# Six fused transformer layers on one core: normalising on another engine, a new order of the first loads, and new stage priorities

## The reference

```
L0:    y = attention(x, ctx, ctx, mask) @ Wo.T + bo + x;  x = (y - mean) * rsqrt(var + 1e-12) * ln_g + ln_b
L1:    y = attention(x, ctx, ctx) @ Wo.T + bo + x;        x = (y - mean) / sqrt(var + 1e-5) * gamma + beta
SELF:  h = LN1(x);  x = x + causal_attention(h, h, h) @ m_proj_w + m_proj_b
CROSS: x = x + attention(LN2(x), ctx, ctx) @ c_proj_w + c_proj_b
FFN:   x = x + relu(LN3(x) @ f_w1 + f_b1) @ f_w2 + f_b2
L3:    x = x + attention(LN4(x), ctx, ctx) @ ternary(Wo).T + bo     (Wq, Wk, Wv ternary too)
```

## Time and profile before

| | us |
|---|---|
| median of three runs | 1471.36 (1467.45 to 1472.52) |
| the profiled execution | 1471.28 |
| span of its profile | 1469.5 |

### The profile page before, as it was taken

How to read it: one execution, slowest core, us unless ns; L and a number is a source line. 1 busy time by engine, 2 the same in 40 slices (tenths; PEclk the granted TensorE clock), 3 DMA queues, 4 the chain that set the end, 5 groups by cost and what they waited for, 6 DMA issues and landing times.

```text
span 1469.5 us, 44720 instructions
## 1 busy us (share of the span) xinstructions
PE 1372.2 (93%) x19500; PEld 1158.0 (79%) x19500; DVE 1093.1 (74%) x2032; ACT 809.8 (55%) x1327; POOL 564.4 (38%) x579
## 2 busy tenths in 40 slices
PE   4899889899989999999999999998999999999998
PEld 4777777777877778787888877787899999788786
DVE  2776777798888876767777798788576666878674
ACT  3667555656656556465555666665433333566654
POOL 5854333544354345233333343122277555212100
PEclk9999999999999999999999999999999999999999
DMA  7211000100000010000000010000000000001000
GB/s 253 69 51 54 26 12 15 36 24 9 9 15 9 2 31 17 2 2 2 2 2 17 9 44 9 8 15 23 1 16 1 1 1 2 23 23 37 24 23 30
DMA packets 17034, 34.94 MB, mean 24 GB/s; under 512 B 2503, under 2 KB 7879, under 8 KB 16327
## 3 DMA queue, kind: packets, MB, share of 16 engines
q1 hardware_dynamic: 16839, 32.09, 7.0%
HBM read 27.89 MB, written 4.19 MB: 22 GB/s over the span
## 4 chain that ended last, share of the span: by engine, by line
PE 66%; DVE 22%; ACT 5%; issue 4%; POOL 1%; DMA 1%; SPq 1%; DVEq 0%; ACTq 0%; POOLq 0%
DVE s_nm L1064 10%; PE ps L690 9%; PE ps L755 8%; PE ps L783 5%; PE ps L769 5%; PE ps L717 5%; PE ps L582 5%; PE ps L635 4%; PE ps L734 4%; PE ps L594 4%; PE ps L607 3%; PE ps L695 2%; DVE s_KH L1021 2%; ACT s_PU L904 2%; PE ps L714 2%
## 5 line engine op out<-in xcount | busy, mean ns | idle before, releaser
L1064 DVE TENSOR_REDUCE s_nm<-ps 128x8 fp32r<-128x960 f32 (+1 forms) x352 | 397.7, 1168 | 75.0 <-PE ps L635 41.9
L904 ACT ACTIVATE s_PU<-ps 120x1024 f32<-120x1024 f32 (+1 forms) x288 | 279.5, 1026 | 144.4 <-PE ps L695 144.3
L1195 POOL TENSOR_TENSOR s_xs<-s_xs,s_rowv 128x512 f32<-128x512 f32 x96 | 125.0, 1302 | 285.6 <-DVE s_nt L984 266.7
L690 PE MATMUL ps<-s_Qs,s_KH 32*120 32x256 f32 (+2 forms) x4608 | 194.8, 293 | 29.4 <-DVE s_nm L1064 16.5
L690 PEld LDWEIGHTS ps<-s_Qs,s_KH 32*120 32x120 f32 (+1 forms) x4608 | 157.4, 183 | 58.0 <-DVE s_nm L1064 20.1
L913 ACT ACTIVATE s_Os<-ps 128x512 f32<-128x512 f32 x160 | 95.1, 597 | 115.6 <-PE ps L717 71.2
L755 PE MATMUL ps<-s_W,s_oT 128*128 128x256 f32 x960 | 137.6, 294 | 6.3 <-DVE s_oT L997 5.2
L582 PE MATMUL ps<-s_xT,s_W 128*128 128x256 f32 x960 | 135.5, 291 | 4.4 <-POOL s_xT L1201 3.0
L717 PE MATMUL ps<-s_PU,s_Vp 120*32 120x256 f32 x2048 | 131.2, 384 | 8.8 <-DVE s_nm L1064 5.8
L755 PEld LDWEIGHTS ps<-s_W,s_oT 128*128 128x128 f32 x960 | 122.5, 194 | 19.3 <-DVE s_oT L997 13.7
L582 PEld LDWEIGHTS ps<-s_xT,s_W 128*128 128x128 f32 x960 | 120.7, 191 | 11.5 <-issue 4.5
(11 more groups left out here) (98 smaller groups left out, 2540.8 us busy)
## 6 DMA issues: line engine op xcount, KB each, us to landing
s_cf<-ctx_t SPq DMA_DIRECT2D x32, 240.0 KB, 2.6
s_ws<-weights SPq DMA_DIRECT2D x28, 256.0 KB, 2.8
s_xs<-x_nat SPq DMA_DIRECT2D x4, 1024.0 KB, 10.8
s_nt<-x_t SPq DMA_DIRECT2D x16, 256.0 KB, 2.7
out<-s_xs SPq DMA_DIRECT2D x16, 256.0 KB, 2.0
s_rowv<-rows SPq DMA_DIRECT2D x6, 512.0 KB, 4.0
s_mi<-mask SPq DMA_DIRECT2D x8, 120.0 KB, 3.4
s_ident<-ident SPq DMA_DIRECT2D x1, 64.0 KB, 1.9
```

The costliest lines, as they stand in the source:

```text
L690: e.matmul(banks[j][0:n, wide * x:wide * x + wide], kz[row[j], lk, g, c, k0:k0 + n], q[row[j], lq, g, qs_], start=(x == 0 and y_ == 0), st ...
L904: t = e.activation(P_of(i, k)[0:n, :, :], pair("B", i, k)[0:n, :, :], ACT.Exp, scale=0.25)
L1064: e.tensor_reduce(o, v, AX.X, ALU.max, negate=True).then_inc(sem["max"])
L1195: e.tensor_tensor(xs[:, b, :, :], xs[:, b, :, :], row2(layer, 0), ALU.add).then_inc(sem["pool"])
```

## The change

- N and ln move from VectorE to ScalarE, as `activation(Identity)` with scale rs and bias -mean * rs: the same two instructions of 128 x 256 for each stage, 192 in all. GpSimd makes the bias in place of the mean, by two more instructions on 128 x 2 in each rs (96 of them): a product and a change of sign.
- The low part of L0's four weights is made by VectorE (stage Wd) instead of GpSimd (Wl).
- The constants are one array and one transfer of 128 x 306; the mask columns are a transfer of their own in SP's planned order, with its own semaphore.
- The wants of the first loads: K's weights first, then the context and the mask, Q's weights, the mask columns, x^T, V's weights, the row vectors, O's weights; the x blocks later than before.
- WANT has a value for each layer for most stages; STAY goes from 0.158 to 0.006; LONG gets values for the moved stages.

The diff, without the parts that follow from these (names of semaphores, dispatch tables, arguments):

```diff
 
 
-WANT = dict(Xl=-1.31, xT=-3, cT=-4, mi=-4, bo=-0.54, N=2.96, T=-0.96, Q=0.18, Qh=2.79, Ql=0.43, K=-0.21, Kh=1.11, Kl=0.59,
-            K0=-0.06, V=0.68, Ve=2.57, mf=-0.74, A=0.45, max=0.14, M=-0.05, mTe=0.55, B=0.86, exp=0.68, cap=1.77, PV=1.79,
-            PVe=2.42, ON=2.33, ONe=1.93, OT=2.98, O=-0.19, y=2.45, st=6.41, rs=0.41, ln=1.69, lng=4.37, F1=-0.76, Fa=0.46,
-            Fv=-2.33, Hl=0.58, F2=2.43, out=2.2, Th=-2.92, Tl=-1.16, OTh=-0.54, OTl=1.4, Ch=-3, Cl=-3)
-
-
-LONG = dict(xT=.6, cT=.6, mi=.6, ws=.6, row=.6, x=.6, out=.6, bo=1.3, N=.65, T=.44, Th=.48, Tl=.62, Xl=1.3, Q=1.43, Qh=.74, Ql=.8, K=1.35, K0=.87,
+WANT = dict(Xl=2.33, xT=-3, cT=-4, mi=-4, bo=(-1.38, -4.6, 0.82, 0.54, 4.02, -2.73), N=(0, 0, 7.36, 5.95, 4.46, 10.15),
+            T=(0, -1.03, -0.22, -0.68, -0.56, -0.75), Q=(0.31, -0.09, 0.08, 0.12, 0, 0.89), Qh=(4.65, 5.69, 4.82, 2.33, 0, 7.3),
+            Ql=(4.24, 5.24, -0.37, 1.41, 0, -4.79), K=(0.04, 0.95, -0.74, -0.32, 0, 0.14), Kh=(7.03, 3.26, 8.4, 3.42, 0, 7.23),
+            Kl=(13.58, 11.97, 2.38, 0.81, 0, 4.94), K0=(-2.55, -0.13, 1.77, -5.48, 0, -4.59), V=(1.53, 1.27, 1.39, 1.09, 0, 0.96),
+            Ve=(7.29, 6, 8.04, 5.94, 0, 5.43), mf=-9.45, A=(0.94, 0.26, -0.22, 0.9, 0, -4.03),
+            max=(1.44, -8.07, -2.39, -8.27, 0, -4.55), M=(-4.4, -9.75, -3.93, -3.85, 0, -3.9), mTe=(-3.16, 5.59, 2.13, -1.13, 0, 8.06),
+            B=(0.16, -1.34, -2.27, -1.09, 0, -3.55), exp=(1.98, 1.72, -0.9, 3.06, 0, 2.4), cap=2.08,
+            PV=(2.68, 2.11, 1.48, 2.16, 0, -0.32), PVe=(2.06, -0.55, 4.1, 4.9, 0, 4), ON=(1.61, 2.48, 3.07, 2.54, 0, -2.38),
+            ONe=(-0.48, -5, -3.72, -3.42, 0, -8.34), OT=(4.03, 1.43, 3.08, 1.76, 0, 3.6), O=(-3.16, -1.62, -1.42, 2.41, 0, 0.38),
+            y=(3.92, 3.63, 1.68, 3.03, 1.58, 1.11), st=(7.15, 8.77, 12.99, 7.5, 9.79, 0), rs=(1.67, -0.61, 1.09, -0.07, 5.79, 0),
+            ln=(11.5, 3.83, 0, 0, 0, 0), lng=(0.08, 5.07, 0, 0, 0, 0), F1=-0.96, Fa=8.14, Fv=8.74, Hl=2.08, F2=1.38, out=2.2,
+            Th=(-5.03, -8.61, -5.12, -8.43, -10, -10.16), Tl=(0, 1.26, -0.81, 1.24, -1.59, 2.94),
+            OTh=(-9.48, -6.82, -11.62, -5.25, 0, -8.56), OTl=(-2.41, 0.77, -6.29, -1.15, 0, -2.19),
+            Ch=(-1.04, -0.8, 0, -8.83, 0, -3.71), Cl=(0.77, -2.69, 0, 0.79, 0, -6.45))
+
+
+LONG = dict(mci=.5, xT=.6, cT=.6, mi=.6, ws=.6, row=.6, x=.6, out=.6, bo=1.3, N=.72, T=.44, Th=.48, Tl=.62, Xl=1.3, Q=1.43, Qh=.74, Ql=.8, K=1.35, K0=.87,
             Kh=1.17, Kl=1.25, V=1.43, Ve=.67, Ch=.5, Cl=1.25, mf=.3, A=.69, max=1.07, M=.22, mTe=.28, B=.95, exp=.91, cap=.67, PV=.87,
-            PVe=.48, ON=.44, ONe=.64, OT=.44, OTh=.48, OTl=.62, O=1.43, y=.6, st=1.05, rs=1.04, ln=.65, lng=2.6, F1=2.86, Fa=.72, Fv=.79,
-            Hl=2.43, F2=2.86, wb=.5, wa=.2, wg=.75, Wh=.52, Wl=1.3, qs=.57, qm=.05, qa=1.5, qw=4.1)
+            PVe=.48, ON=.44, ONe=.64, OT=.44, OTh=.48, OTl=.62, O=1.43, y=.6, st=1.05, rs=1.6, ln=.72, lng=2.6, F1=2.86, Fa=.72, Fv=.79,
+            Hl=2.43, F2=2.86, wb=.5, Wd=.6, wa=.2, wg=.75, Wh=.52, Wl=1.3, qs=.57, qm=.05, qa=1.5, qw=4.1)
 LAND = dict(xT=2.5, cT=2.5, mi=2.5, ws=3.0, row=3.5, x=7.0, out=3.0)
 
 ARRAY = dict(A="rows", B="rows", PV="columns")
 TURN = .19
-STAY = 0.158
+STAY = 0.006
 NEXT = .11
 
 
@@ -54,6 +64,17 @@
 def half_pairs(i, hf):
 
     return [2 * hf, 2 * hf + 1] + ([4, 5] if layer_of(i) == "SELF" else [])
+
+
+def want_of(name, i):
+
+    v = WANT[name]
+    return v[LAYERS.index(layer_of(i))] if isinstance(v, tuple) else v
+
+
+def rest_of(layer):
+
+    return "Wd" if layer == "L0" else "Wl"
...
-                add("DVE", "N", after=[x_ready(i), ("rs", i - B, 1 if layer_of(i - B) == "L1" else 0)],
+                add("ACT", "N", after=[x_ready(i), ("rs", i - B, 1 if layer_of(i - B) == "L1" else 0)],
...
-            add("PE", "Q", after=[x_t, ("Wl", layer, 0)],
+            add("PE", "Q", after=[x_t, (rest_of(layer), layer, 0)],
...
-            add("DVE", "ln", after=[("rs", i, 0)])
+            add("ACT", "ln", after=[("rs", i, 0)])
...
-    p.add("SP", "row", 0, want=-3.5, rings=[("row", 0, layer_end("L0", "lng"))])
-    p.add("SP", "x", 0, want=-3.4)
-    for k in range(1, 4):
-        p.add("SP", "x", k, want=-2 + k)
+    p.add("SP", "row", 0, want=-2.6, rings=[("row", 0, layer_end("L0", "lng"))])
+    p.add("SP", "mci", 0, want=-3.3)
+    for k in range(4):
+        p.add("SP", "x", k, want=-1 + 1.2 * k)
...
-        for m in range(4):
-            at = start + (.5 if n else .05) * m
-            p.add("SP", "ws", layer, m, want=at, rings=[("ws", (layer, m), [("Wl", layer, m)])])
+        for m in (1, 0, 2, 3) if n == 0 else range(4):
+            at = start + .5 * m if n else {1: -9, 0: -3.9, 2: -2.7, 3: -.5}[m]
+            p.add("SP", "ws", layer, m, want=at, rings=[("ws", (layer, m), [(rest_of(layer), layer, m)])])
...
+            if layer == "L0":
+                p.add("DVE", "Wd", layer, m, want=at, after=[("Wh", layer, m)])
+            else:
+                p.add("POOL", "Wl", layer, m, want=at, after=[("Wh", layer, m)])
...
+N_CST = 16
...
+        cst = sb("cst", [128, 306])
+        ident, caus, hsel, pick, colv, c2 = (cst[:, a:b] for a, b in ((0, 128), (128, 256), (256, 258), (258, 262), (262, 282), (282, 306)))
...
+            n_pool += {"bo": 1, "cap": 1, "rs": 4, "lng": 2, "Xl": 1, "Cl": 1, "Hl": 1, "Wl": 1, "qw": 3}[name]
...
+            if n == "L0":
+                return sem["Wd"], nth("Wd", n, m)
...
+            def N(i):
+                was = ring["nt"].before[i]
+                if layer_of(was) == "L0":
+                    w.wait_ge(sem["pool"], pool_ops["Xl", was, 0])
+                else:
+                    w.wait_ge(sem["T"], nth("T", was))
+                w.wait_ge(sem["pool"], pool_ops["rs", i - B, 1 if layer_of(i - B) == "L1" else 0])
+                w.wait_ge(*x_value(i))
+                b = i % B
+                for q in range(2):
+                    t = e.activation(nt[slot("nt", i)][:, q, :], xs[:, b, q, :], ACT.Identity, bias=mv[:, b, q, 0:1],
+                                     scale=rs[:, b, q:q + 1])
+                t.then_inc(sem["N"])
+
+            def ln(i):
+                b = i % B
+                w.wait_ge(sem["pool"], pool_ops["rs", i, 0])
+                for q in range(2):
+                    t = e.activation(xs[:, b, q, :], xs[:, b, q, :], ACT.Identity, bias=mv[:, b, q, 0:1], scale=rs[:, b, q:q + 1])
+                t.then_inc(sem["ln"])
...
+            w.wait_ge(sem["d_mci"], 16)
             e.tensor_scalar(mcol[0:C, :], mci[0:C, :], 0.0, GONE / 4, ALU.is_equal, ALU.mult).then_inc(sem["cst"])
-
-            def N(i):
-                was = ring["nt"].before[i]
-                if layer_of(was) == "L0":
-                    w.wait_ge(sem["pool"], pool_ops["Xl", was, 0])
-                else:
-                    w.wait_ge(sem["T"], nth("T", was))
-                w.wait_ge(sem["pool"], pool_ops["rs", i - B, 1 if layer_of(i - B) == "L1" else 0])
-                w.wait_ge(*x_value(i))
-                b = i % B
-                for q in range(2):
-                    t = e.tensor_scalar(nt[slot("nt", i)][:, q, :], xs[:, b, q, :], mv[:, b, q, 0:1], rs[:, b, q:q + 1],
-                                        ALU.subtract, ALU.mult)
-                t.then_inc(sem["N"])
 
...
+            def Wd(n, m):
+                w.wait_ge(sem["Wh"], nth("Wh", n, m))
+                e.tensor_tensor(wv(n, 1, m), ws_of(n, m)[:, :, :], wv(n, 0, m).bitcast(f32), ALU.subtract).then_inc(sem["Wd"])
...
-            def ln(i):
-                b = i % B
-                w.wait_ge(sem["pool"], pool_ops["rs", i, 0])
-                for q in range(2):
-                    t = e.tensor_scalar(xs[:, b, q, :], xs[:, b, q, :], mv[:, b, q, 0:1], rs[:, b, q:q + 1], ALU.subtract, ALU.mult)
-                t.then_inc(sem["ln"])
...
+                behind()
+                e.tensor_tensor(mv[:, b, :, 0], mv[:, b, :, 0], rs[:, b, :], ALU.mult).then_inc(sem["pool"])
+                behind()
+                e.tensor_scalar(mv[:, b, :, 0], mv[:, b, :, 0], -1.0, None, ALU.mult).then_inc(sem["pool"])
...
-            for tile, src in ((hsel[:, :], headsel_d), (ident[:, :], ident_d), (caus[:, :], causal_d), (pick[:, :], pick_d),
-                              (colv[:, :], cols[:, 0:20]), (c2[:, :], cols[:, 20:44]), (mci[0:C, :], mask_t)):
-                e.dma_start(tile, src).then_inc(sem["d_cst"], 16)
+            e.dma_start(cst[:, :], consts).then_inc(sem["d_cst"], 16)
...
+            def mcols(i):
+                e.dma_start(mci[0:C, :], mask_t).then_inc(sem["d_mci"], 16)
```

More of the change, by code:

```diff
@@ L115, in add @@
         key = (name, i, k)
-        self.stages[key] = Stage(engine, key, at + (WANT[name] if want is None else want), LONG[name] if long is None else long,
+        self.stages[key] = Stage(engine, key, at + (want_of(name, i) if want is None else want), LONG[name] if long is None else long,
                                  list(after), list(rings))
@@ L268, in make_plan @@
```

(21 more changed lines are left out.)

14 lines of the change are left out of this document (3 added, 11 removed).

## The result

The changed kernel takes **1402.71 us** (median of four runs, 1402.28 to 1404.88) against 1471.94: ratio 0.954, 95% interval 0.952 to 0.956. The forecast was 1441 with a range from 1410: right in sign, too small by more than half, and 7 us outside the range. Rival B (1406) had named the time, with a chance of 0.12.

What follows compares the result with a forecast made beforehand. TensorE's own work was taken as the floor, leaving its 97.3 us idle, array turns and lower clock. Terms -10 - 16 + 4 - 10 + 2 = -30 us from 1471 gave 1441, range 1410 to 1466.

Steps and rivals of the forecast that it cites:

- Rival B: Whole kernel: most TensorE waits go; VectorE's relief -35, wants -20, start -10 us, giving 1406 us; chance 0.12.
- Start, -10 us: Kernel start: earlier context and K weights bring first K near 7.5, first scores near 15 us; -10, ends 0 and -16.
- Move, -16 on VectorE and +4 on ScalarE: N and ln: lighter VectorE cuts TensorE's waits, -16 us; ScalarE's added work delays exps and evacuations, +4 us.
- 30% less queueing: VectorE's queue: waiting goes as busy over idle share, 2.8 before and 2.0 after, giving -16 us.
- the 52.3 us of waits: TensorE's waits naming VectorE as releaser, 23 rows summed; expected to fall to near 36 us.
- The +4: ScalarE's queue: waits scaled by load, 2 us, plus some 2 for ln pairs waiting on rs; ends 0 and +33.
- Wants, -10, ends -35 and +20: Compute queues' order: wants by layer save a quarter of the first two layers' idle time, -10 us.
- The +2 for STAY: TensorE's array shapes: lower STAY changes visits little, as most wants lie further apart than 0.158; +2 us.
- Rival A: Whole kernel: only the start pays, VectorE waits being of necessary order; 1461 us, chance 0.18.
- rival C: ScalarE's queue: N or ln pairs ahead of needed exps make it the one to wait for; +11, 1482 us; chance 0.10.

Runs made afterwards that it cites:

- fitted orders: Kernels with wants fitted to their division of work: N, ln on ScalarE, five including the changed kernel, mean 1406.4 us; on VectorE, three, mean 1416.0 us.
- the two searches: New start, old STAY, wants searched from the old ones, two random sequences per engine: N, ln on VectorE 1409.31 and 1422.21 us, on ScalarE 1410.42 and 1405.04.
- the worst misfit: Kernel before with only the new wants by layer and STAY 0.006; old start, N and ln on VectorE: 1520.52 us.
- The table: All eight combinations of start, move and wants (with STAY), each old or new, including the kernels before and after: 1402.7 to 1520.5 us.

## Why the prediction was wrong

**Start, -10 us.** Right in size and mechanism: -8.3 alone and -12.2 on top of move and wants, though only -2.7 beside the move with the old wants. First K at 7.99 (forecast 7.5), scores at 17.76 (15). The difference is the mask columns and the order Q, Q, V before the first scores. What I hadn't looked at is the weight that came late at 26.81.

**Move, -16 on VectorE and +4 on ScalarE.** Here the reasoning failed. The engine sums came near: VectorE 989.0 (forecast 984), ScalarE 897.7 (910), GpSimd 600.0 (622). For ScalarE that is partly luck: an instruction takes 0.60 us and not 0.52, 192 of them are 115 us, and the engine's busy time rose by only 88. The 128 of N alone cover 69.4 us of time instead of 128 x 0.597 = 76: neighbours overlap in the profile. But "30% less queueing" treats VectorE as a queue fed at random, while the engines work off lists that the planner makes anew when a stage changes its engine. With the old wants it made a plan 16 us longer, and the run with the move alone took 2.7 us more, not 12 less; of the 52.3 us of waits, 47.6 remained. The prediction had the relief without the new lists. The relief may be in there: that kernel is 59 us longer than its plan, the one before 73, and beside the new start it is 58 and 66. That would be 14 and 8 us, near the -12 forecast and the 8 to 10 among fitted orders. It is argued from the plan, whose durations of N are themselves wrong (0.65 us where VectorE takes 1.28 for a pair, 0.72 where ScalarE takes 1.08), and no run shows it. The +4 was also scaled by load alone; with the same busy over idle as for VectorE it would have been about +7.

**Wants, -10, ends -35 and +20.** This is the term that was mis-sized, and the main step that failed: beside the move, the new wants are worth -60 and -69 us. Orders from the two searches are worth 54 and 41 us with N on VectorE (1463.6 to 1409.3 and 1422.2) and 67 and 61 with N on ScalarE (1471.9 to 1405.0 and 1410.4), and the worst misfit costs 49. Both ends were too near. I had reasoned from how much idle time one set of wants for all layers leaves, and had taken the coarse reading of the wants, as priorities. I wrote that the new order can't be worked out from the trace; it could be from the kernel. Run without the chip, the planner gives 1398.9 us before and 1354.2 after, 45 us less, where the whole forecast was 30. I had also left out TensorE's busy time as something an order can shorten: it was to stay within 5 us of 1372, and fell by 28.6. The +2 for STAY has no run of its own; its reason, a visit more or less, isn't borne out: the array changes fell from 696 to 652.

**The sum.** The steps were added. The table shows that they can't be: the wants are worth -69 or +48 by what stands beside them. Rival A is out: idle time outside the first 32 us is 42.3 us and not 77. Rival B came within 4 us of the time, but by luck: its 65 us were to be idle time, 35 of them waits for VectorE that the move takes, and 28.6 of the 69.8 came out of the busy time instead; rival C's mechanism, waits for ScalarE, rose from 16.2 to 24.6 us and not to 40. The rule of the Trainium skill, "ScalarE: Activation LUTs", section Rules for kernel authors, that adds and multiplies belong on VectorE, agrees with the median instruction, 0.41 us there against 0.59 on ScalarE. It didn't decide the time: with fitted orders the kernels with N on ScalarE are 8 to 10 us shorter in the mean.

## What to carry to other kernels

Where a kernel's queues are laid out by a planner from fixed durations, an edit of the work and the order of the work can't be priced apart: refit the order for each side of a comparison, or the comparison measures the luck of the order (here 50 us either way, against about 10 for the edit). Run the planner before forecasting; its own length had the sign and most of the size of what a new set of priorities did. When a stage moves to another engine, look at the new lists before crediting the relief. To learn whether a set of tuned priorities means something, shift them all by a tenth of a step: if the gain goes, it was a found order, the next edit can break it, and the search belongs in the build.
